# Mirrored sums: copied out of PSUM by ScalarE and added by GpSimd, and diagonal tiles taken apart in the order of tiles

## The reference, cut to what matters

```python
h = x @ weight
h_norm = h / jnp.maximum(norm, NORM_EPS)
sim = h_norm @ h_norm.T
attn_logits = sim / TAU + jnp.log(adj + EPS)
attn = jax.nn.softmax(attn_logits, axis=1)
out = attn @ h + bias
```

## Time and profile before

| what | us |
|---|---|
| median of 3 runs | 1335.18 |
| the three runs | 1329.08, 1335.18, 1477.92 |
| the profiled execution | 1339.48 |
| its span, first to last instruction | 1337.7 |

### The profile page before, as it was taken

How to read it: one execution, slowest core, us unless ns; L and a number is a source line. 1 busy time by engine, 2 the same in 40 slices (tenths; PEclk the granted TensorE clock), 3 DMA queues, 4 the chain that set the end, 5 groups by cost and what they waited for, 6 DMA issues and landing times.

```text
span 1337.7 us, 26725 instructions
## 1 busy us (share of the span) xinstructions
PE 1271.8 (95%) x9548; PEld 944.0 (71%) x9548; DVE 1012.4 (76%) x2273; ACT 629.6 (47%) x1480; POOL 365.2 (27%) x422
## 2 busy tenths in 40 slices
PE   6999999979999999989999999999999977899998
PEld 4788788854455555557776777777767655688887
DVE  7878789899455555579888978978889988776642
ACT  5654456546223222266656755656656654311111
POOL 2000000012422223213223332332333222465433
PEclk9999999999999999999999999999999999999999
DMA  9999999932111220125653554544544414250500
GB/s 225 247 340 294 307 354 380 382 145 84 48 57 54 63 64 17 48 87 157 198 174 119 174 163 126 173 133 148 177 122 155 135 56 119 79 150 26 150 25 25
DMA packets 122899, 199.93 MB, mean 149 GB/s; under 512 B 13201, under 2 KB 83857, under 8 KB 122769
## 3 DMA queue, kind: packets, MB, share of 16 engines
q1 hardware_dynamic: 115568, 194.04, 47.0%
q10 hardware_dynamic: 7200, 4.20, 1.1%
HBM read 147.85 MB, written 50.33 MB: 148 GB/s over the span
## 4 chain that ended last, share of the span: by engine, by line
PE 55%; issue 13%; DVE 11%; DMA 5%; POOL 4%; ACT 2%; SPq 1%; ACTq 0%; DVEq 0%; POOLq 0%
PE ps L1823 12%; PE ps L1619 8%; PE ps L1620 8%; PE ps L1732 7%; DMA acc<-in_adj 5%; PE ps L1717 5%; PE ps L1718 5%; DVE ring L795 4%; POOL ring L693 3%; PE ps L1784 3%; PE ps L1749 2%; DVE small L807 2%; SPq L431 1%; DVE ring L1043 1%; DVE ring L1073 1%
## 5 line engine op out<-in xcount | busy, mean ns | idle before, releaser
L693 POOL TENSOR_TENSOR ring<-ring 128x512 f16<-128x512 f32 (+3 forms) x133 | 151.9, 1149 | 327.8 <-ACT ring L1493 327.8
L1581 PE MATMUL ps<-val_hi,ring 128*128 128x257 f16 x1024 | 227.2, 274 | 5.0 <-DVE ring L795 5.0
L1582 PE MATMUL ps<-val_lo,ring 128*128 128x256 f16 x1024 | 227.1, 274 | 0.0
L1619 PE MATMUL ps<-ring,acc 128*128 128x512 fp8e4 x512 | 196.7, 384 | 6.7 <-DVE acc L933 6.7
L1732 PE MATMUL ps<-hnt 128*128 128x512 f16 (+3 forms) x864 | 196.3, 363 | 1.0 <-DVE ring L1043 1.0
L1620 PE MATMUL ps<-ring,acc 128*128 128x512 fp8e4 x512 | 196.6, 384 | 0.0
L795 DVE STREAM_TRANSPOSE ring<-acc 128x1024 uint8<-128x1024 uint8 x128 | 151.2, 1219 | 39.1 <-DMA acc<-in_adj 39.0
L1717 PE MATMUL ps<-val_hi,ring 128*128 128x257 f16 x490 | 134.7, 275 | 22.8 <-POOL ring L693 13.9
L1372 ACT ACTIVATE hnt<-ring 128x512 bf16<-128x512 uint8 (+1 forms) x192 | 115.1, 602 | 82.7 <-DVE ring L795 82.7
L1717 PE MATMUL ps<-val_hi,hs 128*128 128x257 f16 x534 | 145.8, 273 | 1.1 <-DVE acc L1106 0.6
L1749 PE MATMUL ps<-val_hi,hs 128*128 128x257 f16 x534 | 145.8, 273 | 0.0
(11 more groups left out here) (234 smaller groups left out, 2371.3 us busy)
## 6 DMA issues: line engine op xcount, KB each, us to landing
acc<-in_adj SPq DMA_DIRECT2D x256, 256.0 KB, 9.3
turned_dram<-ring SPq DMA_DIRECT2D x56, 512.0 KB, 2.9
ring<-turned_dram SPq DMA_DIRECT2D x224, 128.0 KB, 2.9
at_dram<-ring SPq DMA_DIRECT2D x32, 512.0 KB, 9.8
ring<-at_dram SPq DMA_DIRECT2D x64, 256.0 KB, 3.9
ring<-at_dram SPq DMA_DIRECT2D x24, 512.0 KB, 3.8
ring<-at_dram SPq DMA_DIRECT2D x9, 1024.0 KB, 9.7
xs<-in_x SPq DMA_DIRECT2D x12, 256.0 KB, 10.6
```

Of the source, the lines that this page charges most:

```text
L693: nc.gpsimd.tensor_tensor(lo2[m % 2][:, k:GW], p2t[m % 2][:, k:GW], hi2[m % 2][:, k:GW], ALU.subtract).then_inc(sem["lo2_done"], 1)
L1581: nc.tensor.matmul(ps[:, k % 8, 0:D + 1], lhs, val_hi0[:, t, 0:D + 1], start=(t == 0), stop=False)
L1582: last = nc.tensor.matmul(ps[:, k % 8, 0:D], lhs, val_lo0[:, t, :], start=False, stop=(t == NB - 1))
L1619: nc.tensor.matmul(ps[:, bank + c, :], g_hi[:, t, c * P:(c + 1) * P], src, start=(t == 0), stop=False)
```

## The change

- `add_mirror` leaves DVE. In its place ACT's new `mirror_out` copies the sum out of PSUM: in group 0 straight into `acc`, in the others into one of two buffers `mirrored`, which lie in parts of `misc` and `w_all`. It stands behind `weights_high(n + 1)` and ahead of `exps(n + 2)`. POOL's new `add_mirror` adds the buffer to `acc[:, j]`, ahead of the step's `mirror_low`. PE waits for the copy (`acc_copied`) before it writes the bank again, DVE's `group_sum` for copy and adds.
- In groups 1 to 6 the tiles come in the order 0, 4, 5, 1, 6, 7, 2, 3, 8, ...: the diagonal ones stand at places 0, 3, 6 and 7, not at 0 to 3. Groups 0 and 7 keep 0, 3, 1, 2.
- In groups 1 to 6 the mirrored product of an inner tile comes a step later than before (place o + 1). Outer ones still come four steps later.
- Bank 6 is given to every other outer sum only from the group's fifth step on. `group_sum` of groups 1 to 6 waits for the last inner product too, and chunks of adj are loaded when the step that used the buffer last is done, wherever that step now is.

```diff
@@ -125,8 +125,8 @@
         lo2 = [temps[:, 5120 + i * 512:5632 + i * 512].bitcast(F16) for i in range(2)]
-        w_all = sb("w_all", [P, 3 * C * D], F32)
-        w = w_all[:, :].rearrange("p (l c d) -> p l c d", l=3, c=C)
+        w_all = sb("w_all", [P, 3 * C * D + 1], F32)
+        w = w_all[:, 0:3 * C * D].rearrange("p (l c d) -> p l c d", l=3, c=C)
         w1_hi = w_all[:, 0:256].bitcast(F16).rearrange("p (c d) -> p c d", c=C)
@@ -134,9 +134,10 @@
         back = [ring[:, a:a + 2048].bitcast(F32) for a in (7 * N + 2048, 7 * N)]
-        misc = sb("misc", [P, 3 * D], F32)
+        misc = sb("misc", [P, 3 * D + 1], F32)
         xn = [misc[:, i * D:(i + 1) * D] for i in range(2)]
         bias_bc = misc[:, 2 * D:3 * D]
+        mirrored = [misc[:, 2 * D:3 * D + 1], w_all[:, 5 * D:6 * D + 1]]
         hs = sb("hs", [P, 4 * D], F32)
@@ -288,7 +289,14 @@
         mirror_pairs = [p for p in pairs if p[0] != p[1]]
-        order = [(g, g * GB + j) for g in range(NG) for j in (0, 3, 1, 2) + tuple(range(GB, NB - g * GB))]
+        def rows_in(g):
+            if 0 < g < NG - 1:
+                return (0, 4, 5, 1, 6, 7, 2, 3) + tuple(range(2 * GB, NB - g * GB))
+            return (0, 3, 1, 2) + tuple(range(GB, NB - g * GB))
+        order = [(g, g * GB + j) for g in range(NG) for j in rows_in(g)]
         NS = len(order)
@@ -302,7 +310,8 @@
-            return ([n - LAG] if 0 <= n - LAG < NS and outer[n - LAG] else []) + ([n] if n < NS and inner[n] else [])
+            return ([n - LAG] if 0 <= n - LAG < NS and outer[n - LAG] else []) + \
+                [o for o in (n - 1, n) if 0 <= o < NS and inner[o] and o + (order[o][0] < NG - 1) == n]
@@ -312,7 +321,7 @@
             g = order[n][0]
-            return 6 if g > 0 and n_outer[n] % 2 and n + LAG < opens[g + 1] - 1 else 7
+            return 6 if g > 0 and n_outer[n] % 2 and opens[g] + LAG <= n < opens[g + 1] - 1 - LAG else 7
@@ -335,6 +344,18 @@
+        def last_in(c):
+            return max(n for n in range(NS) if chunk_of(n) == c)
+        def mirrored_last(g, b):
+            return any(inner[n] and order[n] == (g, g * GB + b) and n + (g < NG - 1) >= last_step(g, b) for n in range(NS))
+        def last_step(g, b):
+            return max(n for n in range(opens[g], opens[g + 1]) if first_block(n) <= b)
@@ -499,9 +520,9 @@
                 if c >= 3:
-                    sp.wait_ge(sem["p1_done"], GB * (c - 2))
+                    sp.wait_ge(sem["p1_done"], last_in(c - 3) + 1)
                     if 0 < pairs[c - 3][0] == pairs[c - 3][1]:
-                        sp.wait_ge(sem["p2_done"], place[GB * (c - 2) - 1] + 1)
+                        sp.wait_ge(sem["p2_done"], place[max(n for n in range(NS) if inner[n] and chunk_of(n) == c - 3)] + 1)
                 sp.dma_start(chunk1[c % 3], at_t[g, :, t * GB:(t + 1) * GB, :]).then_inc(c1_loaded[c % 3], 16)
@@ -541,7 +562,7 @@
             outer_steps = [n for n in range(NS) if outer[n]]
-            chunk_at = {GB * c - 7: c for c in range(3, len(pairs))}
+            chunk_at = {last_in(c - 3) + 2: c for c in range(3, len(pairs))}
             mirror_chunk_at = {last_of(c - 3) + LAG + 1: c for c in range(3, len(mirror_pairs))}
@@ -693,6 +714,13 @@
+            def add_mirror(n):
+                (g, j), m = order[n], n_outer[n]
+                pool.wait_ge(sem["acc_copied"], m + 1)
+                since(pool, sem["acc_added"], m - NB + (g + 1) * GB - n_outer[opens[1]])
+                nc.gpsimd.tensor_tensor(acc[:, j, :], acc[:, j, :], mirrored[m % 2], ALU.add).then_inc(sem["acc_added"], 1)
@@ -700,11 +728,17 @@
                     root_norm(late_at["project2"][n])
+                for o in mirrors_at(n - 1):
+                    if outer[o] and order[o][0] > 0:
+                        add_mirror(o)
                 for o in mirrors_at(n + 1):
                         root_var3(g)
+            for o in mirrors_at(NS - 1):
+                if outer[o]:
+                    add_mirror(o)
             root_var3(NG - 2)
@@ -1083,26 +1117,17 @@
-            def add_mirror(n):
-                (g, j), m = order[n], n_outer[n]
-                dve.wait_ge(sem["pv2_done"], place[n] + 1)
-                if g == 0:
-                    nc.vector.tensor_copy(acc[:, j, :], ps[:, mirror_bank(n), 0:D + 1]).then_inc(sem["acc_added"], 1)
-                else:
-                    dve.wait_ge(sem["acc_added"], m - NB + (g + 1) * GB)
-                    nc.vector.tensor_tensor(acc[:, j, :], acc[:, j, :], ps[:, mirror_bank(n), 0:D + 1], ALU.add).then_inc(sem["acc_added"], 1)
                 dve.wait_ge(sem["pv1_done"], opens[g + 1])
-                if g == NG - 1:
-                    dve.wait_ge(sem["pv2_done"], NM)
+                if g > 0:
+                    dve.wait_ge(sem["pv2_done"], NM if g == NG - 1 else place[max(n for n in range(opens[g + 1]) if inner[n])] + 1)
                 if g == 0:
                 else:
-                    dve.wait_ge(sem["acc_added"], n_outer[opens[g]])
+                    dve.wait_ge(sem["acc_copied"], n_outer[opens[1]])
+                    since(dve, sem["acc_added"], n_outer[opens[g]] - n_outer[opens[1]])
                     nc.vector.tensor_tensor(acc[:, k, :], acc[:, k, :], ps[:, b, 0:D + 1], ALU.add).then_inc(sem["group_out"], 1)
@@ -1273,15 +1298,8 @@
                     turn(n + 1)
-                for o in mirrors_at(n - 1):
-                    if outer[o]:
-                        add_mirror(o)
                 if n + 1 < NS:
                     weights_low(n + 1)
-                if n == NS - 1:
-                    for o in mirrors_at(n):
-                        if outer[o]:
-                            add_mirror(o)
                 if n in late_at["transposes_n"]:
@@ -1492,6 +1510,18 @@
+            def mirror_out(n):
+                m = n_outer[n]
+                act.wait_ge(sem["pv2_done"], place[n] + 1)
+                if order[n][0] == 0:
+                    to = acc[:, order[n][1], :]
+                else:
+                    act.wait_ge(sem["x_biased"], NB)
+                    since(act, sem["acc_added"], m - 1 - n_outer[opens[1]])
+                    to = mirrored[m % 2]
+                nc.scalar.activation(to, ps[:, mirror_bank(n), 0:D + 1], ACT.Copy).then_inc(sem["acc_copied"], 1)
@@ -1524,6 +1554,9 @@
                     weights_high(n + 1)
+                for o in mirrors_at(n - 1):
+                    if outer[o]:
+                        mirror_out(o)
                 if n in late_at["transposes_n"]:
@@ -1747,7 +1783,7 @@
                     last = nc.tensor.matmul(ps[:, b, 0:D + 1], lo1[n % 2][:, b * P:(b + 1) * P], val_hi0[:, j, 0:D + 1],
-                                            start=False, stop=(j == NB - 1 if g < NG - 1 else n == NS - 1 and b == GB - 1))
+                                            start=False, stop=(n == last_step(g, b) and not mirrored_last(g, b)))
                 last.then_inc(sem["pv1_done"], 1)
@@ -1764,7 +1800,7 @@
                     pe.wait_ge(sem["p2_done"], place[[o for o in range(n) if inner[o]][-1]] + 1)
-                since(pe, sem["acc_added"], sums_in(6, n))
+                since(pe, sem["acc_copied"], sums_in(6, n - 1 - LAG))
                 for b in mirror_blocks(n):
@@ -1774,15 +1810,15 @@
                 if outer[n]:
-                    since(pe, sem["acc_added"], sums_in(bank, n))
+                    since(pe, sem["acc_copied"], sums_in(bank, n))
                     if bank == 6:
-                        pe.wait_ge(sem["p2_done"], place[max(o for o in range(n) if inner[o])] + 1)
+                        pe.wait_ge(sem["p2_done"], place[max(o for o in range(n + LAG + 1) if inner[o])] + 1)
                     if n_outer[n] == 0:
                     last = nc.tensor.matmul(ps[:, bank, 0:D + 1], lo2[m % 2][:, b * P:(b + 1) * P], val_hi0[:, g * GB + b, 0:D + 1],
-                                            start=False, stop=(b == GB - 1 and (outer[n] or g == NG - 1)))
+                                            start=False, stop=(b == GB - 1 and (outer[n] or mirrored_last(g, bank))))
                 last.then_inc(sem["pv2_done"], 1)
@@ -1852,7 +1888,7 @@
             pe.wait_ge(sem["p2_done"], NM)
-            pe.wait_ge(sem["acc_added"], n_outer[NS])
+            pe.wait_ge(sem["acc_copied"], n_outer[NS])
             for n in range(3):
```

More of the change, by code:

```diff
@@ L37 @@
 s2_ready sumsq_ready hi2_ready ss_clamped val2_ready inv_ready hn_ready tn_done hnhi_ready hnt_ready
-s_done exp_raw exp_done turned written p1_done hi1_done lo1_done pv1_done t_done p2_done hi2_done lo2_done pv2_done acc_added
+s_done exp_raw exp_done turned written p1_done hi1_done lo1_done pv1_done t_done p2_done hi2_done lo2_done pv2_done acc_copied acc_added
 group_out rden_ready rsc_ready x3_done stats3_done var3_ready rstd3_ready nm3_ready h3_done hi3_done lo3_done
```

## The result

The change makes the kernel slower by 1%: median 1340.49 us (20 runs) against 1329.02 us of before (20 runs, of which the three shown above are a part), ratio 1.0102 with a 95% interval of 1.0075 to 1.0128. The medians lie 11.5 us apart; the ratio, which leaves out the slow runs of both, stands for 13.6.

What follows compares the result with a forecast made beforehand. PE, busy 95%, was taken as the bound. Full steps 0, DVE +0.3, group 7 -5.5, group 6 +0.3, openings -3.8 sum to -8.7, say -9 us: 1335.2 to 1326 us, range 1311 to 1341.

Steps and rivals of the forecast that it cites:

- Full steps, 0: Full steps in the middle of a group: they stay at 3.93 us, as ACT and POOL have room; 0 us.
- DVE, 6.8 - 6.5 = +0.3: Groups 5 to 7, 19 adds: POOL's adds cost DVE 6.8 us, its removed instruction gives back 6.5; net +0.3 us.
- my 0.36, half of 0.73: DVE time lost to each POOL add, taken as half of the possible 0 to 0.73 us.
- The release of the bank: Bank 7, freed by ACT's copy behind `weights_high`: 0.7 us later at a group 6 opening, priced at 0 in the sum.
- rival C: Bank 7 freed 0.7 us later, up to 20 waits in groups 4 to 7, 14 us: net +5, 1340 us; chance 0.14.
- The order of tiles, -9: Attention groups: group 7 gains 5.5 us, group 6 loses 0.3, groups 1 to 5 gain 3.8 at their openings.
- DVE has 3.93 us a step to keep up with: Openings of groups 1 to 5: mixing in full steps gives DVE 3.93 us a step instead of two or three.
- the new wait in `group_sum`: Groups 1 to 6, DVE waiting for the last inner product: up to 1 us a group, taken as 0.
- Group 7 about 20 us: Sign of being right: group 7's stretch falls from 25.3 us to about 20, forecast 19.8.
- The waits for the copy under 5 us: Sign of being right: PE's waits for the bank, now behind ACT's copy, total under 5 us.
- the first product of the last layer: Sign of being wrong: this product does not come earlier by what the attention gained.
- Group 6, 37.0 us: Sign of being wrong: group 6 longer than 37 us, from 34.8 before.

Runs made afterwards that it cites:

- e2: Changed kernel with copy and add given back to DVE as one instruction, leaving new tile order and later inner products: attention 557.2 us, ratio 1.0038.
- e5: Changed kernel with ACT's copy ahead of `weights_high` and POOL's adds of groups 1 to 7 left out (sums dropped): attention 548.1 us, ratio 0.9952.
- e3: Changed kernel with ACT's copy ahead of `weights_high` instead of behind it, POOL still adding: attention 557.4 us, ratio 1.0035.
- e4: Changed kernel without POOL's adds in groups 1 to 7, the copy still behind `weights_high` (sums dropped): attention 559.7 us, ratio 1.0023.
- e12: Changed kernel with sums given back to DVE and the previous group's tail three steps later in groups 1 to 4: attention 551.4 us, ratio 0.9970.

## Why the prediction was right or wrong

**Full steps, 0: right where they are full.** `scores` starts every 3.93 us after as before; ACT and POOL had the room. Group 0, with its 28 copies on ACT, takes 122.0 us, as before.

**DVE, 6.8 - 6.5 = +0.3: near in the sum, in part by luck.** Its two sides were larger and mostly in another place. Relief: e2 to e5, DVE's add out of PSUM gone and nothing in its place but an early copy, is -9.1 us. Price: the adds on POOL are +9.3 (e5 to e3) or +9.6 (e4 to after). I had put both into groups 5 to 7 with their 19 adds and nothing into groups 1 to 4. Of the relief only 1.9 us are in groups 5 to 7 and 7.5 in groups 1 to 4, of the price 3.6 and 5.7 to 6.0. In time of DVE's an add costs 0.44 us behind the late copy and 0.30 behind the early one, and my 0.36, half of 0.73, lies between. So an add doesn't take its whole length from DVE. The Trainium skill's page "SBUF — State Buffer" (section "SBUF: two separate sides") speaks of an exclusive lock for a whole instruction; the trace agrees in kind, since L1084 and L1107 get shorter as soon as the adds are gone (e4, e5), and the mean price of 0.44 us stands beside the 0.96 us that an add mostly lasts.

**The release of the bank: the step that failed.** I saw it (rival C: "0.7 later") and priced it at 0 in the forecast, since "PE has 2.6 us of other work between two such products". After less e3 and e4 less e5 measure it: 11.9 and 11.6 us, in size most of the 13.9, with 7.7 and 7.4 of them in groups 1 to 4 at full clock. My argument counted PE's work between two products and not how late `weights` is: in an opening DVE took 5.9 us for a step (803.31 less 797.4), more than PE's 3.9 to 4.3, and the copy inherited all of that. Most of this lateness comes from the order: e2, with nothing moved off DVE, takes 5.4 us for the same step, before 4.0. Rival C's mechanism is the right one. That its bound of 14 us was close is partly luck: it had up to 20 places at 0.7 us in groups 4 to 7, and there were 11 waits of 0.6 to 2.1 us, with over half of the loss in groups 1 to 4. Its price was net +5, because I set the order's 9 us against it.

**The order of tiles, -9: wrong.** Alone it is +1.8 (e2). Behind group 4 it gives 4.3 (103.3 to 99.0), where I had 5.5 - 0.3 + 0.8 = 6.0: right in kind. In groups 1 to 4 I forecast -3.0 and it costs 6.1. The sentence that failed is "DVE has 3.93 us a step to keep up with": at places 1 to 3 a full step's work, the mirrored product, the group sums and the tail come to more than that, 5.44 us from one `weights` to the next in e2's group 2. e12 shows which part decides: there the same step takes 3.72 us, and with the tail out of the way the openings are 0.8 us shorter than before's. The table of the tail, which I left where it was, belonged to the old order. A smaller part is the new wait in `group_sum`, which I took at 0: in group 2 DVE stands 1.6 us for PE there in e2 and 0.6 in before.

**The sum.** From before over e2, e5 and e4 to after: +1.8 (order) - 9.1 (relief) + 11.6 (late release) + 9.6 (adds) = 13.9 in the attention. As each term is the difference of two neighbours, that they add up proves nothing; what speaks for them is that the last two come out nearly alike by way of e3 (9.3 and 11.9). The forecast had -9 for the first and 0 for the late release. The time itself lies just inside the range, since the three runs that it stood on were 6 us above the median of the twenty; in its direction the forecast was wrong.

**What I named as signs.** Full steps at 3.93: seen. DVE as busy as before with fewer instructions: seen, busier. L1050 and L1073 longer on average: seen, 704 to 834 and 305 to 363 ns. Group 7 about 20 us: 22.9. The waits for the copy under 5 us: 15.8. Of the signs of being wrong one came: the first product of the last layer lies 13.9 us later from the attention's start. Group 6, 37.0 us, stands at the bound of another.

## What to carry to other kernels

Where a buffer is freed by an instruction that moves to another engine, ask what stands ahead of it there and what that waits for: the copy was no slower, but it had inherited the latest engine's delay, and its place in ACT's list was worth 12 us (7 in the old order). A GpSimd add beside a VectorE that works from SBUF took 0.30 to 0.44 us of VectorE's time, about the 0.40 that it had spared. When an order is leveled by hand, move the work that was laid out by step numbers with it: the same order cost 1.8 us with the old table of the tail and gave 4.0 with a shifted one.

## What the hardware showed unexpectedly

The granted clock fell in group 7 after, though PE's longest wait there was as long as before's. The two waits, before and after, and PE's busy time and granted clock in stretches of after:

```profile
1113.41 0.28 PE L1717 MATMUL ps<-val_hi,ring 128*128 128x257 f16 x1 [2.92 <-POOL ring L693]
...
1117.78 0.28 PE L1753 MATMUL ps<-val_hi,ring 128*128 128x257 f16 x1 [2.92 <-POOL ring L714]
```

```profile
1111.00:1114.00 3.00, 1.75 (x12) 1.08 (x13) 2.30 (x6) 1.77 (x5) 0.96 (x1) 1.00 0.00 0
1114.00:1117.00 3.00, 0.86 (x8) 0.52 (x6) 2.91 (x11) 1.10 (x3) 1.22 (x1) 1.00 0.02 5
...
1119.00:1122.00 3.00, 3.00 (x16) 2.12 (x15) 1.06 (x3) 1.35 (x3) 1.16 (x1) 0.51 0.00 0
```

From 1118.6 on the same matmuls start 0.215 us apart, not 0.11 (granted 0.51, the level of 1.2 GHz), until 1122; between 1125 and 1131 it is 0.72. In the earlier trace rows the clock of group 7 is 1.00, through waits of 2.92 and 2.79 us. In group 6 it fell too, at 1081.0 in after, behind a wait of 2.46 us, and at 1076.8 in e2, behind one of 1.93 us. So in this kernel the longest wait alone doesn't tell whether the clock falls. Nor does it follow from PE having less to do in group 7 (two mirrored products had moved out), since e2 has the same order and keeps its clock there:

```profile
1100.00:1123.00 23.00, 15.53 (x129) 11.57 (x127) 18.91 (x55) 11.30 (x27) 7.15 (x7) 1.00 0.05 14
```

Group 7 took 22.9 us for the 19.8 forecast. How much of the 3.1 is the clock no run here separates.

POOL's add takes 0.64 us at the least (L722, min), less than the 0.73 that I had from its add of 256 columns; its median is 0.96. That it is longer because it too waits for DVE is my reading.
